# One rounded type for the six transposes of a step, and the mixed tiles' last weights by transfers from DRAM

## The reference, cut to what matters

```
logits = x @ router_weight.T                      # 32 experts
topv, topi = top_k(softmax(logits), 4);  topv /= sum(topv)
g = einsum('th,ehf->etf', x, w_gate)              # h 256, f 96
u = einsum('th,ehf->etf', x, w_up)
act = silu(g) * u
out = einsum('te,etf,efh->th', combine, act, w_down)
shared = silu(x @ sw_gate) * (x @ sw_up) @ sw_down
out = out + sigmoid(x @ sgate_w) * shared
```

## Time and profile before

| | |
|---|---|
| median of 3 runs | 617.88 us (616.66 to 620.54) |
| the profiled execution | 619.86 us, its span 618.1 us |
| mean granted clock of PE | 0.982 |
| busy, share of the span | PE 93%, PE weight loads 72%, DVE 57%, ACT 40%, POOL 51% |

### The profile page before, as it was taken

How to read it: one execution, slowest core, us unless ns; L and a number is a source line. 1 busy time by engine, 2 the same in 40 slices (tenths; PEclk the granted TensorE clock), 3 DMA queues, 4 the chain that set the end, 5 groups by cost and what they waited for, 6 DMA issues and landing times.

```text
span 618.1 us, 13183 instructions
## 1 busy us (share of the span) xinstructions
PE 575.5 (93%) x3980; PEld 442.3 (72%) x3980; DVE 351.4 (57%) x1153; ACT 249.7 (40%) x628; POOL 314.6 (51%) x531
## 2 busy tenths in 40 slices
PE   7999999999998798999999889999999898979997
PEld 6999889888985554658777667777778675556464
DVE  4576677657754565423445445455455545189985
ACT  4555445444543121013566555456555543101110
POOL 3114878877887588840455545555565456500000
PEclk9999999999998888899999999999999999989999
DMA  6965645555442393234555554555555442398844
GB/s 189 300 230 187 233 159 167 201 169 162 153 164 105 96 243 110 90 98 106 136 148 153 142 147 139 156 155 151 155 163 158 126 140 85 119 396 313 299 174 136
DMA packets 65907, 104.35 MB, mean 169 GB/s; under 512 B 9808, under 2 KB 52816, under 8 KB 65744
## 3 DMA queue, kind: packets, MB, share of 16 engines
q1 hardware_dynamic: 48112, 63.62, 35.1%
q0 software_dynamic: 12672, 35.14, 15.5%
q10 hardware_dynamic: 5056, 4.75, 2.5%
HBM read 59.84 MB, written 43.65 MB: 167 GB/s over the span
## 4 chain that ended last, share of the span: by engine, by line
PE 67%; issue 11%; ACT 7%; another core or an unknown queue 6%; DVE 5%; DMA 1%; ACTq 1%; SPq 0%; POOL 0%; DVEq 0%; POOLq 0%
PE bank L677 15%; PE bank L670 12%; PE bank L891 7%; PE bank L699 6%; PE bank L918 5%; PE bank L772 4%; PE bank L887 3%; PE bank L724 2%; PE bank L817 2%; PE bank L901 2%; PE bank L863 2%; ACT hnt L601 2%; PE bank L915 1%; ACT att_split L509 1%
## 5 line engine op out<-in xcount | busy, mean ns | idle before, releaser
L480 POOL DMA_INDIRECT returned<-arena,back x136 | 132.0, 971 | 132.8 <-DVE arena L1288 70.6
L436 POOL DMA_INDIRECT sent<-rows,slot x128 | 128.5, 1004 | 23.6 <-issue 22.7
L677 PE MATMUL bank<-hnt,ws_gu 128*128 128x512 f32 x256 | 121.0, 624 | 2.5 <-DVE slot_prod L1106 2.5
L677 PEld LDWEIGHTS bank<-hnt,ws_gu 128*128 128x128 f32 x256 | 50.7, 200 | 59.5 <-issue 54.4
L891 PE MATMUL bank<-w_gu,arena 128*128 x416 | 84.5, 339 | 3.0 <-ACT arena L573 1.7
L1288 DVE TENSOR_TENSOR arena<-bank,arena 128x192 f32<-128x192 f32 x68 | 24.2, 356 | 86.0 <-ACT arena L579 69.8
L891 PEld LDWEIGHTS bank<-w_gu,arena 128*128 128x128 f32 x416 | 65.8, 189 | 4.3 <-issue 4.0
L573 ACT COPY arena<-bank 128x512 f32<-128x512 f32 x68 | 39.4, 581 | 65.9 <-PE bank L863 45.7
L499 ACT ACTIVATE act_t<-bank 128x512 f32<-128x512 f32 x28 | 16.6, 597 | 116.7 <-PE bank L677 104.5
L863 PE MATMUL bank<-ident_r,loaded 128*128 128x128 f32 x272 | 57.1, 297 | 0.0
L601 ACT COPY hnt<-w_gu 128x384 f32 x128 | 56.0, 514 | 0.0
(11 more groups left out here) (179 smaller groups left out, 944.0 us busy)
## 6 DMA issues: line engine op xcount, KB each, us to landing
arena<-returned SPq DMA_DIRECT2D x16, 1024.0 KB, 6.2
loaded<-sent SPq DMA_DIRECT2D x104, 132.0 KB
w_gu<-w_gate_up SPq DMA_DIRECT2D x16, 384.0 KB
sent<-rows SPq DMA_DIRECT2D x1, 4224.0 KB, 15.8
loaded<-sent SPq DMA_DIRECT2D x128, 33.0 KB
resid<-x SPq DMA_DIRECT2D x16, 256.0 KB
att_plain<-ctx_t SPq DMA_DIRECT2D x16, 256.0 KB
att_plain<-ctx SPq DMA_DIRECT2D x16, 256.0 KB
```

Of the source, the lines that this page charges most:

```text
L436: pool.indirect_dma_start(out=sent, out_offset=bass.IndirectOffsetOnAxis(ap=slot[:, 2 * b + j, k:k + 1], axis=0), in_=rows[:, u, j, :], in ...
L480: pool.indirect_dma_start(out=returned, out_offset=bass.IndirectOffsetOnAxis(ap=back[:, t:t + 1], axis=0), in_=down_e[u][:, s, :], in_offs ...
L677: last = pe.matmul(bank[:, :], ws_gu[:, c, at:at + P], hnt[:, c, 512 * g:512 * g + 512], start=(c == 0), stop=(c == DC - 1))
```

## The change

Four edits that belong together:

- `expert_act_transpose` reads the activations through `act_e_r`, a view of the same memory as `act_e` typed f32r, and the identity `ident_r`. So the six transposes of a step are of one type.
- `copy_down` of ACT and of DVE, and DVE's reading of the table for it, are gone.
- SP gets `load_down(pair)`: it reads four words of `tile_expert`, waits for `down_psum` as the copies did, and issues four transfers of 96 rows of 1 KB (96 KB each) from `w_down` in DRAM to `dn_copy`. They stand in SP's list behind `load_tiles` of five pairs later, and ahead of `load_tiles` of six pairs later.
- PE waits once, for `dn_copied`, where it waited for both engines' copies.

```diff
+        act_e_r = [w_lo_all[:, 1024 + 192 * n:1216 + 192 * n].rearrange("p (s f) -> p s f", s=2)
+                   for n in range(2)]
...
-            for pair in range(pairs):
+            def load_tiles(pair):
                 u = pair % RING
                 first, size = column_of(pair), QUARTER if mixed(pair) else P
...
+            def load_down(pair):
+                first = column_of(pair)
+                _, named = nc.values_load_multi_w_load_instructions(
+                    tile_expert[0:1, first:first + 4], engines=[mybir.EngineType.SP],
...
+                if pair == FIRST_MIXED:
+                    sp.wait_ge(S["su_psum"], FB * EARLY)
+                wait(sp, "down_psum", pair - 1 if pair > FIRST_MIXED else 0)
+                for q in range(4):
+                    sp.dma_start(dn_copy[:, q, :],
+                                 w_down[:, bass.ds(named[q], 1), :].rearrange("f e d -> f (e d)")) \
+                        .then_inc(S["dn_copied"], 16)
+
+            for pair in range(pairs + 5):
+                if pair < pairs:
+                    load_tiles(pair)
+                if mixed(pair - 5):
+                    load_down(pair - 5)
...
-            def copy_down(pair):
...
-                for q in (2, 3):
-                    last = act.copy(dn_copy[:, q, :], w_dn[:, bass.ds(copied_e[pair][q], 1), :]
-                                    .rearrange("f e d -> f (e d)"))
-                last.then_inc(S["dn_copied_act"], 1)
...
-                    last = pe.transpose(b_v[0:F, P * s:P * s + P],
-                                        act_e[pair % 2][:, s, :], ident[:, :])
+                    last = pe.transpose(b_v[0:F, P * s:P * s + P].bitcast(F32R),
+                                        act_e_r[pair % 2][:, s, :], ident_r[:, :])
...
-                    wait(pe, "dn_copied_act", mixed_until(pair))
-                    wait(pe, "dn_copied_dve", mixed_until(pair))
+                    wait(pe, "dn_copied", 64 * mixed_until(pair))
...
-                for q in (0, 1):
-                    last = dve.tensor_copy(dn_copy[:, q, :], w_dn[:, bass.ds(copied_e[pair][q], 1), :]
-                                           .rearrange("f e d -> f (e d)"))
-                last.then_inc(S["dn_copied_dve"], 1)
...
-                if mixed(pair - 2):
-                    if (pair - 2 - FIRST_MIXED) % 4 == 0:
-                        experts_to_copy(pair - 2)
-                    copy_down(pair - 2)
```

More of the change, by code:

```diff
@@ L225, in build_xattn_moe @@
             "act_et_psum", "act_et_ready", "down_psum", "down_ready",
-            "gu_copied", "ident_ready", "dn_copied_act", "dn_copied_dve",
+            "gu_copied", "ident_ready", "dn_copied",
             "meant_ready", "meant_no_ready", "back_to_ready", "back_ready",
@@ L355, in _ @@
                 sp.dma_start(loaded[:, u, 1, :].bitcast(F32), sent[bass.ds(at[P // size], P), :]).then_inc(tile_in[u], 16)
+            def load_down(pair):
+                first = column_of(pair)
+                _, named = nc.values_load_multi_w_load_instructions(
+                    tile_expert[0:1, first:first + 4], engines=[mybir.EngineType.SP],
+                    min_val=0, max_val=EXPERTS - 1,
+                    skip_runtime_bounds_check_because="a tile's first row over the rows of a region "
+                                                      "is the number of an expert")
+                if pair == FIRST_MIXED:
[10 more added lines that the diff above has]
+                    load_down(pair - 5)
             sp.wait_ge(S["down_psum"], pairs)
@@ L604, in copy_gate_up @@
                 last.then_inc(S["gu_copied"], 1)
-            def copy_down(pair):
-                if pair == FIRST_MIXED:
-                    act.wait_ge(S["down_w"], 16)
-                wait(act, "down_psum", pair - 1 if pair > FIRST_MIXED else 0)
-                for q in (2, 3):
-                    last = act.copy(dn_copy[:, q, :], w_dn[:, bass.ds(copied_e[pair][q], 1), :]
-                                    .rearrange("f e d -> f (e d)"))
-                last.then_inc(S["dn_copied_act"], 1)
             act.wait_ge(S["tables_ready"], 9)
```

## The result

The changed kernel is slower: 671.7 us (666.7 to 672.7, 5 runs) against 620.5 us of the kernel before (616.7 to 626.3), 1.082 times with a 95% interval of 1.076 to 1.089. The profiled execution took 671.8 us with a span of 670.1 us, 52.0 us more than before.

What follows compares the result with a forecast made beforehand. PE was taken as the bound, SP right behind; SP's period of 6.5 + 2.9 = 9.4 us over 28 periods adds 62.8 us to 619.86, giving 682.7, or 681 us against the median. The range was 640 to 709 us.

Steps and rivals of the forecast that it cites:

- second bound: Expert stage: SP works about 6.5 us of every 7.16 us period, right behind PE, which is busy for 94%.
- The size of the period: Expert stage: SP's period becomes 6.5 + 2.9 = 9.4 us, over 28 periods 62.8 us more.
- The added work: SP's list, per mixed pair: a reading of 0.9 us and four transfers, together 2.9 us, bounds 2.7 and 4.5.
- The work of before: SP's list before the change: 6.5 us a period, 5.2 in quiet and 1.3 for POOL's four indirect transfers.
- quiet price: SP's list while POOL isn't yet writing: 2 + 5 transfers without a wait, 5.2 us a period.
- rival 1: SP's list issues at its quiet rate: 8.1 us a period, 644 us, from 639 to 658; chance 0.11.
- SP's room: SP's waiting time in a period before the change: 0.4 to 1.2 us, taken as 0.7.
- The transposes: PE's six transposes of one type take 0.63 us a step, a gain of 2 us in all at most.
- The copies: ACT and DVE lose 64 copies each; PE gains 5 us, bounds 0 and 10.8, hidden while SP is the bound.
- Rival 2: PE's mixed product: only the weights' landing is late, 0 to 0.3 us a period, 618 to 626 us; chance 0.04.
- Rival 3: SP's added work fits into its waits and PE gains: 613 us, 607 at best; chance 0.04.
- Rival 4: PE, idle a third of each period, falls to the lower clock: up to 95 us more, 710 to 776; chance 0.06.

Runs made afterwards that it cites:

- e3: Changed kernel with two of the four transfers of weights per mixed pair left out; 615.2 us, 1.065 times the kernel before.
- e12: Changed kernel without SP's reading of the table for the weights, the transfers at fixed addresses; 628.8 us, 1.083 times the kernel before.
- e5: Changed kernel with transfers of weights half as wide, rows of 512 B in place of 1 KB; 644.4 us, 1.118 times the kernel before.
- e6: Changed kernel with a second buffer for the weights, transfers still in SP's list; 642.7 us, 1.115 times the kernel before.
- e9: Changed kernel with ACT issuing the transfers of weights two steps earlier than in e4, into two buffers; 623.0 us, 1.002 times the kernel before.
- e1: Kernel before with only the transposes of the activations put in the rounded type, copies kept; 575.7 us, 0.998 times the kernel before.
- e4: Changed kernel with the transfers of weights moved from SP's list to ACT, without SP's reading; 625.5 us, 1.083 times the kernel before.
- e8: Kernel before with all four copies of weights on ACT and none on DVE; 583.5 us, 1.011 times the kernel before.
- e7: Changed kernel plus two DVE copies within SBUF per mixed pair, to a place nothing reads; 646.0 us, 1.118 times the kernel before.
- e2: Changed kernel with the transposes of the activations back in f32, so the transfers alone; 647.0 us, 1.120 times the kernel before.
- e11: Changed kernel, unchanged, run again on the chip of the later experiments; 666.9 us, 1.077 times the kernel before.

## Why the prediction was right, and what was off

**The direction and the cause.** The step that decided was that SP is a second bound just behind PE and that its list is in order. The changed kernel shows SP with 0.7 us of waits in 249 us and PE waiting at the tiles' transposes, and e3 and e12 show the time falling with the number of issues and with the reading, e5 and e6 that bytes and the wait don't move it, and e9 that the same transfers in another place, and without their reading, cost no more than the copies did to within 6 us. 681 us was given and 671.7 measured.

**The size of the period** was the term that was off: 9.4 us forecast, 8.90 measured, 28 x 0.5 = 14 us. The added work was put at 2.9 us and is 3.21. The work of before was put at 6.5 us, 1.3 of it for POOL's transfers, and is 3.96 + 1.66 = 5.62 in the changed kernel, near the quiet price of 5.2. So rival 1 was half right: SP issues nearly at its quiet rate. Two readings made the 6.5 too high. SP's room was put at 0.7 us a period and is 0.89 by the records of its sequencer. And the 1.3 us were taken to come again, but SP issues quicker in the changed kernel: from the first start to the last end of the five loads it takes 3.02 us on the mean before (the earlier trace rows has 3.27), 2.70 after. POOL's transfers are as many in both, so they can't be the whole of what slowed SP before; what is, stays open (below). That 671.7 came so near 681 owes something to these errors going opposite ways: the added 0.3 us took back a part of the 0.9.

**The transposes.** 0.63 us forecast, 0.62 measured; 2 us at most, 1.3 measured in e1. That the first two are slow when they come from a product also shows: behind L930 they take 434.60 - 434.29 = 0.31 us, behind a stall 439.96 - 439.79 = 0.17.

**The copies.** That their removal is hidden as long as SP is the bound held. What it is worth by itself no run shows: e9 has them gone and ACT's issues in their place, and comes out even.

**Rival 2** (only the landing) didn't decide, but its price was too low: 0 to 0.3 us a period in the prediction, 7.89 - 6.38 = 1.5 us in e4, where the issues on ACT also come later than they did in the sum. The landing, estimated from transfers of 128 KB at 1.8 us, was 2.4 to 5.0 us there.

**Rival 3** is out. **Rival 4** happened in its first half: the granted clock of the stretch fell to 0.90, once PE stood up to 4 us at a time. It cost nothing that can be seen, because PE's work, even with some of it at half the clock, stayed below SP's period (204 us busy in 249). My reading of one long stall with the clock at 1.00 didn't carry over to stalls that return in every period.

**DVE's copies and POOL.** By the rule of the Trainium skill (SBUF — State Buffer, section "SBUF: two separate sides") that was weighed in the prediction, the removal of DVE's copies would have helped POOL's transfers. Those took 0.965 to 0.992 us before and take as long after (the row below). In e8, without DVE's copies, they take 0.965 to 0.978 us, and in e7, with such copies beside the changed kernel, 0.965 to 1.080 at a median of 0.969. No run here shows the lock:

```profile
L504 POOL DMA_INDIRECT returned<-arena,back x136: 967/972/979, 295.4 to 586.7; - x136
```

**What would be best.** No version of transfers beats the copies; the transposes alone (e1) are 0.2% faster than the kernel before, with an interval (0.996 to 0.999) that just excludes no change.

## What to carry to other kernels

An engine that only issues transfers has no busy column, so add up its list: readings of tables, waits and issues, per period of the loop, and hold the sum against the period of the bound engine. Here an issue costs about 0.5 us of the issuer, for 32, 96 or 128 rows alike, and 7 issues and two readings already filled 5.6 us or more of 7.2. Before work goes from engines with room to a queue, ask what stands behind it in that queue; the same four transfers cost 49 us in SP's list and, against the copies they replace, at most 6 us on ACT, issued two steps ahead into a second buffer and without a reading of their own.

## What the runs showed of the hardware

- A transfer of 96 rows costs its issuer as much with rows of 512 B as with 1 KB (periods of 8.74 and 8.80 us in e5 and e2) and nearly as much with fixed addresses as with registers (four take 1.87 us at the median in e12 and in e2, 1.91 and 2.17 on the mean).
- The same kernel took 576.5 us in three sessions and 620 us in two. The slow sessions lose in every stage, and SP's issues are spread wider (2.9 us in place of 2.6 for five loads). By the runs' records the quick sessions were on chips 0 (e1 to e4), 5 (e5 to e8) and 1 (e12) and the slow one of e9 to e11 on chip 7; the first session's chip isn't named. So it can be the chip, but no run separates chip from session, and what differs was not found. The changed kernel's stage of experts hardly differs between them (8.80 us a period in e2, 8.90 in the first session), so what PE loses to stalls in the slow sessions disappears behind SP.
- The waits view of an engine that only issues can miss waits: it gives SP 10.5 us in the kernel before, where the records of its sequencer have 24.9 us between readings and the waits behind them.
